# Decoder with a state-space stage on one core: gate product moved to ScalarE and GpSimd, an opening product one step later, expert tokens ahead of the quantised weights, diagonals ahead of the experts

## The chip, the core and the metric

The kernel runs on one core of a Trainium2 chip. A core has five engines that work side by side and meet only at semaphores: TensorE (PE in the rows: matrix products; PEld is its load of weights), VectorE (DVE), ScalarE (ACT), GpSimd (POOL) and SyncE (SP, which only issues DMAs). SBUF is the working memory of 128 partitions, PSUM the eight banks of 128 x 512 fp32 that TensorE writes. The metric is the time of one execution on the device in microseconds, as the median of several runs.

## The reference

Two decoder layers over x of 4 x 512 x 256 in fp32 (4 batches of 512 tokens), each sublayer followed by a norm without gain:

```python
x = ln(x + attention16(x))                  # 16 heads of 64, one zero key added
x = ln(x + cross_attention16(x, ctx, mask)) # 16 heads of 16
x = ln(x + experts(x))                      # 8 experts, 2 per token, 256 -> 1024 -> 256
x = ln(x + state_space(x))                  # 4 layers, below
x = ln(x + decoder_block(x, ctx))           # attention to itself alone, cross attention 8 heads, MLP
x = ln(x + quantised_ffn(x))                # weights to -1, 0, 1; activations to 8 bits
```

The state-space stage, which the larger part of the change is about, does in each of its 4 layers:

```python
h = rms(x, norm_w)
xi, z = split(h @ W_in.T)                   # 512 channels each
xc = silu(conv_b + sum(xp[:, k:k+L] * conv_w[:, k] for k in range(4)))
delta, Bm, Cm = split(xc @ W_x.T)           # 64, 16, 16
delta = softplus(delta @ W_dt.T + b_dt)
A = -exp(A_log)
hs = scan(exp(delta * A), delta * xc * Bm)  # over the 512 tokens, 16 states a channel
y = sum over states (hs * Cm) + D * xc
x = x + (y * silu(z)) @ W_out.T
```

The quantised weights are `clip(round(w * s), -1, 1) / s` with `s = 1 / mean(|w|)`.

## The kernel before

The program is one list of instructions an engine, in the order of the code; each waits for counters (semaphores) that other engines raise. Nothing is scheduled by a planner: the order is that of the Python loops.

**Stages.** First both attentions, batch by batch; then the experts, 39 tiles of 128 tokens in a loop (`expert`), whose weights of 3 MB each come in by three buffers; then the gathering of the experts' outputs and norm 2 of the reference, a batch at a time (`ln(b, 2)`); then the state-space stage; then the last block and the quantised part.

**Between attention and experts.** VectorE sums the raw quantised weights `w_raw` (L1865), TensorE adds the sums over partitions (L1316), VectorE takes the means (L1868), scales and rounds `w_raw` in place (L1872, twelve instructions, and L1874). ScalarE then casts them to bf16 (L887 twice, L888). These weights are used only at the very end. TensorE transposes the first 128 expert tokens into bank 4 (L1321), ScalarE copies them to `x_T` (L893), and TensorE starts the first expert (L1337 the two products, L1347 the product down).

**The state-space stage.** A sequence is one batch in one layer: 16 sequences, `i` = 0 to 15. Each has 32 steps `w`, one for each of 16 states and each half (`hf`) of the 512 channels; `W` counts steps through all sequences. In a step VectorE multiplies delta times xc by B (L1934, from PSUM bank 6 into banks 4 and 5) and scans (L1940); ScalarE makes the decays three steps ahead (L1035); GpSimd multiplies the state by C (L773, which waits for the scan); TensorE adds the product to y in banks 0 to 3 by the identity (`add_up`, L1450, two steps behind the scans) and spreads B of the next state over the partitions into bank 6 at odd steps (`spread`, L1435, which waits until both B products of the last state are done). Banks 0 and 1 hold y of half 0, banks 2 and 3 that of half 1; a sequence's y is opened by `D * xc`, a product with a diagonal matrix (`direct`, L1443).

**What runs beside it.** While sequence `i` is scanned, the engines prepare sequence `i + 1` (`start_of`: convolution as products with diagonals L1393, projections L1403, delta products L1410, z products L1364; on ScalarE and GpSimd the softplus as a series, GpSimd's L726 to L741) and the norm and first projection of `i + 2` (`opening`), and finish sequence `i - 1` (`end_of`: output product L1425 at steps 8, 10, 13, 18; `residual` L1956 on VectorE). All of it goes through bank 7. The last two sequences have no opening beside them and the last no `start_of`.

**The border of two sequences.** y of sequence `i - 1` is complete after its steps 30 and 31, which TensorE adds at steps 0 and 1 of sequence `i`. VectorE's `gated` (L1950) multiplies it by silu(z) from PSUM straight into `m_sz`, two instructions behind step 0 and two behind step 1. Only then may `direct(i, hf)` open the banks anew, at steps 1 and 2; and the output product of step 8 waits for `m_sz`.

**The diagonals.** GpSimd makes them from the identity: `conv_weights` (L708, four for each of four channel groups) and `direct_weights` (L713). For layer 0 they stand behind the gathering of the experts' outputs, for later layers beside sequences 2, 6 and 10.

## Time and profile before

| what | value |
| --- | --- |
| time, median of 3 runs | 4558.01 us (4556.92 to 4558.54) |
| the profiled execution's own time, its span | 4549.7 us, 4548.0 us |
| TensorE busy | 3853.8 us, 85% |
| VectorE busy | 3084.3 us, 68% |
| ScalarE busy | 2298.5 us, 51% |
| GpSimd busy | 2283.6 us, 50% |
| scan stage, first to last scan | 1891.1 to 3845.1 us |
| expert loop | 1333.6 to 1758 us |
| TensorE's granted clock over the execution | 0.935 of full |

Busy shares are averages over stages with different limits, so they don't say what bounds a stage. In rows with times, the first number is the start in us from the span's beginning, the second the length; `[1.50 <-PE PS L1450]` means that the engine was idle for 1.50 us before and that TensorE's line 1450 released it. `x2` after an operation merges that many. AR is the large SBUF tensor from which nearly all tiles are cut, PS is PSUM. TensorE has two clock levels, 1.2 and 2.4 GHz; a granted clock of 1.00 is the upper one.

### The profile page before, as it was taken

How to read it: one execution, taken by the hardware profiler on the slowest of the kernel's cores; microseconds unless marked ns; L12 is line 12 of the kernel's file. 1: busy time of each engine (PE TensorE's matmuls, PEld its weight loads, DVE VectorE, ACT ScalarE, POOL GpSimd, SP SyncE). 2: the span in 40 equal slices, each digit the busy share in tenths (PEclk: the TensorE clock that was granted, in tenths of full speed). 3: DMA queues.
4: the chain of work that ended last, by engine and by line, in shares of the span. 5: the costliest groups of instructions: out<-in, count | busy, mean ns of one | idle time of the engine just before them, and what ended most of it. 6: DMA issues, size and time to landing. Idle time of an engine off the chain costs nothing.

```text
span 4548.0 us, 47995 instructions
## 1 busy us (share of the span) xinstructions
PE 3853.8 (85%) x15752; PEld 2039.0 (45%) x15760; DVE 3084.3 (68%) x4131; ACT 2298.5 (51%) x4201; POOL 2283.6 (50%) x1206
## 2 busy tenths in 40 slices
PE   7878878888759996699999999999999987887786
PEld 3443443443449995233333333343433333444443
DVE  3465456446551112499999999999999998546546
ACT  3454455445432222566676666666666663332332
POOL 2353344335320004488888787778887785230220
PEclk9999999999979998899999999999999999788788
DMA  6000000000048885111111111111111121000000
GB/s 221 19 6 11 19 7 10 19 15 1 10 175 313 317 312 176 30 35 35 46 36 39 35 48 33 40 35 35 48 35 38 35 91 33 1 10 12 8 1 10
DMA packets 102383, 272.99 MB, mean 60 GB/s; under 512 B 9776, under 2 KB 55728, under 8 KB 96400
## 3 DMA queue, kind: packets, MB, share of 16 engines
q1 hardware_dynamic: 97216, 256.75, 16.9%
q0 software_dynamic: 4944, 13.51, 0.9%
q8 instruction: 110, 1.80, 0.2%
q14 instruction: 113, 0.93, 0.1%
HBM read 237.32 MB, written 32.90 MB: 59 GB/s over the span
## 4 chain that ended last, share of the span: by engine, by line
PE 36%; POOL 18%; DVE 18%; issue 17%; ACT 9%; SPq 1%; DMA 0%; POOLq 0%; DVEq 0%; ACTq 0%
POOL AR L672 11%; DVE AR L1940 8%; PE PS L1450 7%; PE PS L1337 6%; DVE PS L1934 4%; PE PS L1393 4%; POOL AR L773 3%; PE PS L1347 3%; PE PS L1169 3%; PE PS L1364 3%; ACT AR L1035 2%; PE PS L1177 2%; PE PS L1196 2%; PE PS L1209 2%; PE PS L1443 1%
## 5 line engine op out<-in xcount | busy, mean ns | idle before, releaser
L773 POOL TENSOR_TENSOR AR<-AR 128x1024 f32<-128x1024 f32 x512 | 1215.5, 2378 | 415.1 <-DVE AR L1940 338.8
L1940 DVE TENSOR_TENSOR_SCAN AR<-AR,PS 128x1024 f32<-128x1024 f32 x512 | 1170.5, 2286 | 17.6
L672 POOL TENSOR_TENSOR AR<-AR,rden 128x1024 f32<-128x1024 f32 x320 | 605.4, 1893 | 1051.0 <-DVE rden L1671 985.1
L1450 PE MATMUL PS<-AR,ident 128*128 128x512 f32 x2048 | 1022.7, 627 | 33.1 <-POOL AR L773 33.1
L1035 ACT ACTIVATE AR<-AR,mcol 128x511 f32<-128x511 f32 x1024 | 668.1, 712 | 141.2 <-DVE AR L1940 138.9
L1934 DVE TENSOR_TENSOR PS<-AR,PS 128x1024 f32<-128x1024 f32 x512 | 627.9, 1226 | 78.7 <-PE PS L1435 59.7
L1450 PEld LDWEIGHTS PS<-AR,ident 128*128 128x128 f32 x2048 | 370.8, 193 | 479.7 <-issue 412.3
L1209 PE MATMUL PS<-ident,AR 128*128 128x128 f32 x2560 | 376.5, 294 | 156.7 <-POOL AR L672 90.2
L1209 PEld LDWEIGHTS PS<-ident,AR 128*128 128x128 f32 x2560 | 299.9, 150 | 405.4 <-issue 218.6
L827 ACT ACTIVATE AR<-PS,nm 128x512 f32<-128x512 f32 x384 | 260.0, 682 | 315.6 <-DVE nm L1696 219.9
L1196 PE MATMUL PS<-AR 32*128 32x512 f32 (+1 forms) x1280 | 315.9, 705 | 45.1 <-ACT e L830 11.6
L1660 DVE COPY AR<-PS 128x512 f32<-128x512 f32 x320 | 220.4, 689 | 112.8 <-PE PS L1209 111.2
L1337 PE MATMUL PS<-AR 128*128 128x128 f32 x2496 | 287.3, 276 | 8.2 <-ACT AR L893 8.2
L1169 PE MATMUL PS<-AR 128*128 128x512 f32 x608 | 282.8, 623 | 13.2 <-ACT AR L807 4.5
L1337 PEld LDWEIGHTS PS<-AR 128*128 128x128 f32 x2496 | 286.9, 193 | 10.5 <-ACT AR L893 8.6
L1364 PE MATMUL PS<-AR 128*128 128x512 f32 x512 | 259.3, 631 | 30.8 <-ACT AR L1013 23.8
L1177 PE MATMUL PS<-AR 128*128 128x256 f32 (+1 forms) x896 | 236.8, 424 | 32.5 <-DVE AR L1734 18.0
L837 ACT ACTIVATE AR<-PS 128x512 f32<-128x512 f32 x320 | 188.9, 590 | 137.6 <-PE PS L1209 137.6
L1231 PE MATMUL PS<-AR 128*32 128x256 f32 (+1 forms) x2048 | 255.7, 451 | 2.3 <-DVE AR L1660 1.2
L1393 PE MATMUL PS<-AR 128*128 128x512 f32 x512 | 242.2, 596 | 7.6 <-ACT AR L939 3.3
L1882 DVE TENSOR_TENSOR AR<-PS,AR 128x512 f32<-128x512 f32 x78 | 54.0, 692 | 271.3 <-ACT AR L902 271.3
L1689 DVE CUSTOM_DVE_ANT_0 AR<-PS,AR 128x512 f32<-128x512 f32 x256 | 169.3, 683 | 100.6 <-PE PS L1196 99.4
(259 smaller groups left out, 4674.4 us busy)
## 6 DMA issues: line engine op xcount, KB each, us to landing
AR<-in_xw SPq DMA_DIRECT2D x39, 3072.0 KB, 10.5
AR<-mid_cs SPq DMA_DIRECT2D x256, 256.0 KB, 3.3
mid_xs<-AR SPq DMA_DIRECT2D x32, 512.0 KB, 7.8
AR<-mid_xs SPq DMA_DIRECT2D x39, 128.0 KB, 9.7
mid_ys<-AR POOLq DMA_DIRECT2D x39, 128.0 KB, 7.9
AR<-in_ctx SPq DMA_DIRECT2D x8, 512.0 KB, 5.0
AR<-in_mask SPq DMA_DIRECT2D x4, 1024.0 KB, 5.3
mid_x<-AR SPq DMA_DIRECT2D x8, 512.0 KB, 3.0
```

Of the source, the lines that this page charges most:

```text
L672: pool.tensor_tensor(probs[:, i % 4], probs[:, i % 4], rden[:, i % 4, :].rearrange("p (q o) -> p q o", o=1).to_broadcast([P, 2, 512]), ALU ...
L773: pool.tensor_tensor(m_HC[:, W % 3], m_H[:, W % 3, :].rearrange("p (c s) -> p c s", c=2), m_cb[:, n % 4:n % 4 + 1, :].to_broadcast([P, 2, ...
L1035: ins = act.activation(m_dA[:, W % 4, c, 1:512], m_dl[i % 2][:, cc, 1:512], ACT.Exp, scale=mcol[:, i // B, at:at + 1])
L1169: ins = pe.matmul(PS[:, place(PJ, b, u, 4), :], w[:, k, c * P:(c + 1) * P], xT[:, k, :], start=k == 0, stop=k == kc - 1)
L1196: ins = pe.matmul(PS[:, 2 * (e % 2) + q, :], qT[r:r + wide, h // per, t * P:(t + 1) * P], kT[r:r + wide, h // per, :], start=True, stop=True)
L1209: ins = pe.transpose(PS[:, 4 + q, c * P:(c + 1) * P], probs[:, k % 4, q, c * P:(c + 1) * P], ident[:])
L1337: ins = pe.matmul(PS[:, bank, f * P:(f + 1) * P], w[:, kc, f0:f0 + P], x_T[:, kc, :], start=kc == 0, stop=kc == KC - 1)
L1364: ins = pe.matmul(bank, mWin[:, k, c * P:(c + 1) * P], m_hT[:, k, :], start=k == 0, stop=k == KC - 1)
L1393: ins = pe.matmul(bank, dgc[:, 4 * c + k, :], m_xi[:, c, k:k + 512], start=k == 0, stop=k == 3)
L1450: ins = pe.matmul(PS[:, 2 * hf + c, :], ident[:], m_HC[:, W % 3, c, :], start=False, stop=n == NS - 1)
L1934: v.tensor_tensor(PS[:, 4:6, :], m_du[i % 2][:, 2 * hf:2 * hf + 2, :], PS[:, 6:7, :].to_broadcast([P, 2, 512]), ALU.mult).then_inc(d_bx, 1)
L1940: v.tensor_tensor_scan(m_H[:, W % 3, :], m_dA[:, W % 4].rearrange("p c s -> p (c s)"), PS[:, 4:6, :].rearrange("p c s -> p (c s)"), 0.0, A ...
```

## The change

1. **Gate.** VectorE's `gated` goes. ScalarE's new `taken_y` copies two banks of y into SBUF (128 x 1024), one half ahead of its other work of step 1 and one of step 2, into `m_t` (for the last two sequences into a delta buffer). GpSimd's new `gated` multiplies it into `m_sz`, behind its C products of steps 3 and 4. TensorE's `direct` waits for the copies (`d_yc`), its output product for GpSimd. Behind the last sequence both run without cover.
2. **Opening product.** `direct(i, 1)` goes from step 2, behind `add_up`, to step 3, behind `spread` and ahead of `add_up`.
3. **First expert tokens.** ScalarE copies `x_T` for the first expert ahead of the three casts. TensorE waits before the first expert no longer for the casts but for the means (`wmean_ok`), which have been read from bank 0.
4. **Diagonals** of layer 0 are built by GpSimd right behind the last scatter of tokens, ahead of the expert loop.
5. **Norms** of batches 2 and 3: ScalarE's roots go from steps 6 and 7 of the first preparation to steps 9 and 10, behind the first SiLU (`silus(-1)` at step 8).

```diff
+        y_of = lambda i: m_t if i < N_ITEM - 2 else m_dl[N_ITEM % 2]
...
+            for c in range(CI):
+                conv_weights(0, c)
+            direct_weights(0)
+
             with pool.Fori(0, NT_MOE // 3) as j:
...
-            for c in range(CI):
-                conv_weights(0, c)
-            direct_weights(0)
+            def gated(i, hf):
+                h2 = slice(2 * hf, 2 * hf + 2)
+                if hf == 0:
+                    pool.wait_ge(d_sz, i + 1)
+                pool.wait_ge(d_yc, 2 * i + hf + 1)
+                z = m_sz[i % 2][:, h2, :]
+                pool.tensor_tensor(z, z, y_of(i)[:, h2, :], ALU.mult).then_inc(d_yz, 1)
+
...
                     weighted(N_STEP * i + w)
+                    if i > 0 and 3 <= w < 5:
+                        gated(i - 1, w - 3)
...
+            for hf in range(2):
+                gated(N_ITEM - 1, hf)
...
+            token_T(0)
+
             act.wait_ge(q_rnd, 1)
             for c in range(KC):
                 act.activation(wgu[:, c, :], w_raw[:, 2 * F * c:2 * F * (c + 1)], ACT.Identity, bias=nround[:, 0:1])
...
-            token_T(0)
...
                 if w == 15 and j > 0:
                     act.wait_ge(d_delta, 2 * j)
+                    act.wait_ge(d_yz, 2 * i)
...
+            def taken_y(i, hf):
+                if i < N_ITEM - 2 and hf == 0:
+                    act.wait_ge(d_lin, 2 * (i + 2))
+                if i == N_ITEM - 1:
+                    act.wait_ge(d_yz, 2 * i)
+                act.wait_ge(d_y, N_STEP * (i + 1) - 1 + hf)
+                act.activation(y_of(i)[:, 2 * hf:2 * hf + 2, :], PS[:, 2 * hf:2 * hf + 2, :], ACT.Copy).then_inc(d_yc, 1)
...
-                if w == 6:
-                    ln(2, 2)
-                if w == 7:
-                    ln(3, 2)
                 if w == 8:
                     silus(-1)
+                if w in (9, 10):
+                    ln(w - 7, 2)
                 opening(-1, w)
...
+                    if i > 0 and 1 <= w < 3:
+                        taken_y(i - 1, w - 1)
...
+            for hf in range(2):
+                taken_y(N_ITEM - 1, hf)
...
-            pe.wait_ge(dve_set, 2)
+            pe.wait_ge(wmean_ok, 1)
...
-                        pe.wait_ge(d_yz, 4 * i)
+                        pe.wait_ge(d_yz, 2 * i)
...
                 if i:
-                    pe.wait_ge(d_yz, 4 * i - 2 + 2 * hf)
+                    pe.wait_ge(d_yc, 2 * i - 1 + hf)
...
+                    if w == 3:
+                        direct(i, 1)
                     if W >= 2:
                         add_up(W - 2)
-                    if 1 <= w < 3:
-                        direct(i, w - 1)
+                    if w == 1:
+                        direct(i, 0)
...
             own.link(v.tensor_scalar(wmean[:, 0:3], PS[:, 0, 0:3], 1.0 / (F * D), 1e-5, ALU.mult, ALU.max))
+            v.sem_inc(wmean_ok, 1)
...
-                for c in (2 * hf, 2 * hf + 1):
-                    v.tensor_tensor(m_sz[i % 2][:, c, :], PS[:, c, :], m_sz[i % 2][:, c, :], ALU.mult).then_inc(d_yz, 1)
...
-                    if i > 0 and w < 2:
-                        gated(i - 1, w)
...
-            for hf in range(2):
-                gated(N_ITEM - 1, hf)
```

**TensorE at the border of two sequences.** Before, from the spread of step 1 (L1435); L1450 is `add_up`, L1443 `direct`, L1393 the convolution:

```order
L1435 MATMUL PS<-AR,sel 128x512
L1450 MATMUL PS<-AR,ident 128x512 x2
L1443 MATMUL PS<-AR 128x512 x2
L1393 MATMUL PS<-AR 128x512 x2
L1450 MATMUL PS<-AR,ident 128x512 x2
L1443 MATMUL PS<-AR 128x512 x2
L1393 MATMUL PS<-AR 128x512 x2
L1435 MATMUL PS<-AR,sel 128x512
L1450 MATMUL PS<-AR,ident 128x512 x2
L1393 MATMUL PS<-AR 128x512 x2
```

And in the changed kernel, where the same four have lines 1461, 1476, 1469 and 1419:

```order
L1461 MATMUL PS<-AR,sel 128x512
L1476 MATMUL PS<-AR,ident 128x512 x2
L1469 MATMUL PS<-AR 128x512 x2
L1419 MATMUL PS<-AR 128x512 x2
L1476 MATMUL PS<-AR,ident 128x512 x2
L1419 MATMUL PS<-AR 128x512 x2
L1461 MATMUL PS<-AR,sel 128x512
L1469 MATMUL PS<-AR 128x512 x2
L1476 MATMUL PS<-AR,ident 128x512 x2
L1419 MATMUL PS<-AR 128x512 x2
```

The second `direct` has moved behind the next spread; six groups between two spreads have become five, and the next stretch has five instead of four.

**ScalarE at the start of the experts.** Before, L887 and L888 being the casts and L893 the copy of the tokens:

```order
L863 ACTIVATE g_t<-g_t 128x32
L887 ACTIVATE wgu<-AR,nround 128x2048 x2
L888 ACTIVATE wdn<-AR,nround 128x2048
L893 ACTIVATE AR<-PS 128x256
L906 UNCONDITIONAL_BRANCH
```

And in the changed kernel, with lines 908, 909 and 902:

```order
L878 ACTIVATE g_t<-g_t 128x32
L902 ACTIVATE AR<-PS 128x256
L908 ACTIVATE wgu<-AR,nround 128x2048 x2
L909 ACTIVATE wdn<-AR,nround 128x2048
L921 UNCONDITIONAL_BRANCH
```

The copy stands ahead of the three casts; the Silu of the first expert still stands behind them.

**ScalarE at the front of the scan stage.** Before: L968 copies the convolutions, L816 is a norm's root, L1019 the SiLU, L922 the squares of the next norm, L973 the copy of the projection:

```order
L968 ACTIVATE AR<-PS,mcol 128x512 x2
L816 ACTIVATE std<-mv,epsc 128x4 x2
L968 ACTIVATE AR<-PS,mcol 128x512
L1019 ACT_TABLE_LOAD
L1019 ACTIVATE AR<-AR 128x2048
L1023 ACT_TABLE_LOAD
L922 ACTIVATE AR,ss<-AR 128x256 x4
L924 ACT_TABLE_LOAD
L924 ACTIVATE rms<-ss,epsc 128x4
L925 ACT_TABLE_LOAD
L973 ACTIVATE AR<-PS 128x512
```

And in the changed kernel, with lines 983, 831, 1035, 937 and 988:

```order
L983 ACTIVATE AR<-PS,mcol 128x512 x3
L1035 ACT_TABLE_LOAD
L1035 ACTIVATE AR<-AR 128x2048
L1039 ACT_TABLE_LOAD
L831 ACT_TABLE_LOAD
L831 ACTIVATE std<-mv,epsc 128x4 x2
L937 ACTIVATE AR,ss<-AR 128x256 x4
L939 ACTIVATE rms<-ss,epsc 128x4
L940 ACT_TABLE_LOAD
L988 ACTIVATE AR<-PS 128x512
```

Both roots stand behind the SiLU; the number of table loads is the same, one of them has moved ahead of the roots.

## Rows read from the trace of the kernel before

**Rows 1.** One stretch: length, then busy (count) by engine, PE clock, DMA, GB/s.
```profile
2134.00:2256.00 122.00, 111.96 (x271) 47.16 (x270) 116.66 (x75) 80.61 (x122) 105.73 (x59) 0.99 0.18 47
```

**Rows 2.** Timeline, VectorE: start, length, engine, line, operation, [idle <-releaser], us.
```profile
2133.80 1.29 DVE L1950 TENSOR_TENSOR AR<-PS,AR 128x512 f32<-128x512 f32 x2 [1.50 <-PE PS L1450]
...
2135.01 1.22 DVE L1934 TENSOR_TENSOR PS<-AR,PS 128x1024 f32<-128x1024 f32 x1
...
2147.52 1.23 DVE L1934 TENSOR_TENSOR PS<-AR,PS 128x1024 f32<-128x1024 f32 x1 [0.57 <-PE PS L1435]
```

**Rows 3.** Timeline, TensorE, the same border.
```profile
2136.28 0.39 PE L1435 MATMUL PS<-AR,sel 64*128 64x512 bf16 x1 [0.87 <-DVE PS L1934]
...
2147.10 0.39 PE L1435 MATMUL PS<-AR,sel 64*128 64x512 bf16 x1
...
2154.48 0.39 PE L1435 MATMUL PS<-AR,sel 64*128 64x512 bf16 x1
```

**Rows 4.** Chain of waits, two pieces: start, length, what.
```profile
1833.63 1.71 ACT AR L922 x8
...
2162.29 1.24 DVE PS L1934
```

**Rows 5.** Groups of instructions: busy us, mean ns | idle before.
```profile
L773 POOL TENSOR_TENSOR AR<-AR 128x1024 f32<-128x1024 f32 x484 | 1148.9, 2378 | 374.3 <-DVE AR L1940 300.5 <-PE PS L1450 73.8
...
L939 ACT ACTIVATE AR<-PS 128x512 f32<-128x512 f32 x55 | 32.9, 598 | 126.4 <-PE PS L1364 126.4
```

**Rows 6.** Timelines, last border and stage end.
```profile
3732.57 0.39 PE L1435 MATMUL PS<-AR,sel 64*128 64x512 bf16 x1 [2.59 <-DVE PS L1934]
...
3730.08 1.29 DVE L1950 TENSOR_TENSOR AR<-PS,AR 128x512 f32<-128x512 f32 x2 [0.36 <-PE PS L1450]
...
3849.60 1.29 DVE L1950 TENSOR_TENSOR AR<-PS,AR 128x512 f32<-128x512 f32 x2 [2.22 <-PE PS L1450]
```

**Rows 7.** Timeline, start of the experts; last row, landing of their loads L516.
```profile
1332.97 0.36 ACT L893 ACTIVATE AR<-PS 128x256 f32<-128x256 f32 x1
...
1333.57 9.58 PE L1337 MATMUL PS<-AR 128*128 128x128 f32 x64 [8.16 <-ACT AR L893]
...
1339.69 1.28 ACT L902 ACT_TABLE_LOAD   x1 [6.36 <-PE PS L1337]
...
1343.20 3.62 PE L1347 MATMUL PS<-AR 128*128 128x256 f32 x16
...
DMA to landing us min/median/max: 10.0/10.5/16.4
```

**Rows 8.** VectorE beside GpSimd: line L1923, then timeline rows.
```profile
L1923 DVE TENSOR_SCALAR AR<-AR x32: 667/667/2000, 1846.5 to 3685.7; 128x1024 f32<-128x1024 f32 x32
...
1813.71 1.75 DVE L1640 TENSOR_SCALAR AR<-AR,mv,rstd 128x256 f32<-128x256 f32 x4
...
1821.43 1.38 DVE L1640 TENSOR_SCALAR AR<-AR,mv,rstd 128x256 f32<-128x256 f32 x4
...
1319.01 4.84 DVE L1872 TENSOR_SCALAR AR<-AR,wscale 128x1024 f32<-128x1024 f32 x12
...
1323.88 3.36 DVE L1874 TENSOR_SCALAR AR<-AR 128x6144 f32<-128x6144 f32 x1
```

**Rows 9.** Timeline, front of the scan stage.
```profile
1803.26 9.30 POOL L708 TENSOR_SCALAR AR<-ident,mcol 128x128 f32<-128x128 f32 x16
...
1805.76 5.37 PE L1393 MATMUL PS<-AR 128*128 128x512 f32 x8 [2.04 <-POOL AR L708]
...
1811.91 3.70 PE L1393 MATMUL PS<-AR 128*128 128x512 f32 x8 [0.78 <-ACT AR L968]
...
1820.88 0.30 ACT L816 ACTIVATE std<-mv,epsc 128x4 f32<-128x4 f32 x1
...
1828.22 0.30 ACT L816 ACTIVATE std<-mv,epsc 128x4 f32<-128x4 f32 x1 [7.04 <-DVE mv L1634]
...
1838.25 0.60 ACT L973 ACTIVATE AR<-PS 128x512 f32<-128x512 f32 x1
```

31 lines of the change are left out of this document (14 added, 17 removed).

## The prediction, on record before the run

> **What bounds the kernel now.** I read four things in this order. The page's slices show a scan stage, from 1890 to 3845 us of the span of 4548, in which TensorE, VectorE and GpSimd are all nearly full. The table by stretches gives one sequence of it [rows 1]: of 122 us VectorE is busy 116.7 and TensorE 112.0, so two engines are within 5 us of each other, and which one is late must be read place by place. Then the two timelines around step 0 of a sequence [rows 2, 3], and the chain of waits, which says who had it there [rows 4].
>
> The scans follow each other at about 3.6 us a step. At the border of two sequences VectorE stops for the gate products L1950: idle 1.50 us until TensorE's sum of step 30 is there, then a pair that moves what follows by 1.21 us (2133.80 to 2135.01), and a second pair like it one step on [rows 2]. Taken alone that is 3.9 us a sequence. But VectorE waits for TensorE again at step 4 (0.57 us, for L1435), and by the chain TensorE holds the path there and hands it to VectorE only at step 8, at 2162.29 [rows 2, 4]. TensorE's own rows show why [rows 3]: from L1435 of step 1 at 2136.28 it runs without idle to L1435 of step 3 at 2147.10 (10.82 us: the spread and six groups of some 1.72), and 7.38 us to the next, against about 7.2 us that VectorE needs for two steps. TensorE's only idle there is 0.87 us before step 1's spread, where it waits for the VectorE product behind the gate. The same 0.87 stands at all 14 borders with full TensorE work.
>
> **The gate and the second opening product.** VectorE loses 64 instructions; ScalarE gets 32 copies out of PSUM and GpSimd 32 products. TensorE's work stays: its opening product for the second half goes behind step 3's spread, so the stretch from step 1 to 3 becomes 9.1 us and the next 9.1, together 18.2 as now (10.82 + 7.38). What goes is only the idle before step 1: 14 x 0.87 = 12.2 us. The rest of VectorE's freed time turns into longer waits for L1435 at steps 4 and 6 (by the same sums some 1.7 and 2 us).
>
> The last border, into a sequence with no convolutions beside it, is different: TensorE idles 2.59 us there and VectorE leads [rows 6]. There the whole gate counts: 0.36 + 1.21 + 1.21 = 2.8 us.
>
> At the end of the stage nothing covers the longer route. Now the last gate pair takes 1.29 us [rows 6]; then it is copy plus product. The copy of two banks is bounded below by a copy of one (0.60) and above by two (1.20), the product is as wide as L773, 2.38 [rows 5]. I take 1.20, since the copy's time follows its width in these rows: 3.6 against 1.3, 2.3 us lost (bounds 1.7 and 2.3).
>
> What hides the rest. ScalarE's copies stand in its queue before the decays of steps 4 and 5, which run three steps ahead; the sum that the second waits for ends about 2137.7, so the decay of step 5 is done by 2143, and its scan comes at 2149. If that lead of 6 us were gone, each border would pay the copy, 1.2. TensorE reads the freed banks behind the sum of step 31, when the first copy is done, and at step 3 for the second. GpSimd's products at steps 3 and 4 stand before the C products L773, 2.38 us each in a step of 3.6: slack 1.2 us a step, caught up by step 9, and TensorE asks for those products two steps late. The output product at step 8 waits for the gate of step 4. Scan stage: 12.2 + 2.8 - 2.3 = 12.7 us gained.
>
> **First expert tokens ahead of the quantised weights.** Their copy L893 stands in ScalarE's queue behind three casts and starts at 1332.97; TensorE, idle for 8.16 us since it transposed the tokens, starts at 1333.57 [rows 7]. Moved ahead, the copy runs at 1325.4, right behind the transposition, and TensorE 7.5 us earlier. Its weights are there: the first expert's load is issued before the tokens' own, and the slowest load of the stage takes 16.4 us [rows 7], which is early enough for the next ones too. The casts still end at 1333.0; then come the table load (1.28), Silu (0.60), VectorE's product, and TensorE's L1347 at about 1335.8 instead of 1343.20. So 7.4 us at most.
>
> Two things eat from it. First, the diagonals run on GpSimd while VectorE quantises. VectorE's wide tensor_scalar L1923 takes 0.667 us, but once, beside a GpSimd product, 2.00; and four L1640, beside four of the very diagonals in question, took 1.75 us where four take 1.38 alone [rows 8]. That is 0.37 lost in 1.38. Quantising is 4.84 + 3.36 = 8.2 us [rows 8], so by the same ratio 2.2 us; the bounds are nothing, and one GpSimd instruction (0.60) before each of the 12 narrow ones, 7.2. I take 2.2, since it comes from these two kinds side by side. Second, TensorE now has a gap between its early products and L1347, and it fell to the 1.2 GHz level after a gap before: L1393 took 5.37 us instead of 3.70 after idle of 2.04 [rows 9]. Between nothing and 1.7; I take 0.8, the gap being near 2 again. Left: 4.4 us, bounds 0 and 7.4. The expert loop behind is TensorE without idle, so the gain is carried through it.
>
> The Trainium skill, "SBUF — State Buffer", section "Who interferes with whom", says that a VectorE instruction in a two-port mode (tensor_scalar may take one) and a GpSimd instruction exclude each other for a whole instruction. The 2.00 us row agrees with a full block; the L1640 rows show far less, 0.37 us for four. By the rule in full the expert gain would be nearly nil, which is rival 3.
>
> **Diagonals ahead of the experts.** 16 + 4 instructions of 0.60 us leave the front of the scan stage. TensorE's first convolution waits 2.04 us for the first four; a gap behind a ScalarE copy is 0.78 there, so it starts 1.3 us earlier. It may also stay at the high level, 1.7 us more [rows 9].
>
> **Norms 2 and 3 behind the first SiLU.** Now ScalarE idles 7.04 us for norm 3 before the last convolution copy at 1828.42 [rows 9]. After the change the copies and the SiLU pass at once, but the roots wait: last copy at about 1823.2 instead of 1828.4, SiLU done at 1827, two table loads, root 2 at 1829.7 instead of 1820.88. From root 2 to root 3 VectorE needs 7.34 us (1820.88 to 1828.22), so root 3 comes at 1837.1, and only then its 0.30, the squares 1.71 [rows 4], a root of 0.30, a table load 1.28 and copy L973 at 1840.7, against 1838.25 now. Late by 2.5 us, or by 0.9 if the first convolution stays fast. TensorE, idle for longer, then starts the delta products at the low level: up to 1 us more. Bounds 0.9 and 3.5 lost; I take the middle, 2.2. The 7 us of idle are not removed but moved behind the SiLU.
>
> **Sum.** 12.7 + 4.4 - 2.2 = 14.9 us off the profiled execution's 4549.7, giving 4534.8. The runs' median is 8.3 above that execution, so 4558.0 - 14.9 = 4543.1.
>
> **Rivals.**
> 1. TensorE is not the bound at the border and the whole gate counts: 15 x 3.9 = 59 us, 4499. For it: the idle is put down to the gate. Against: TensorE's gapless 18.2 us and the chain.
> 2. The two stage fronts cost their upper bounds: TensorE's clock falls wherever a gap is new, experts gain 0.5 and the norms lose 3.5, and one more dip costs the scans some us: 12.7 + 0.5 - 3.5 = 9.7 at best, 4548 to 4553.
> 3. The port excludes for whole instructions: quantising 7.2 us later, expert gain 0.2: 12.7 + 0.2 - 2.2 = 10.7, 4547.
> 4. Slower: GpSimd does not catch up. Its delta products from step 20 on already delay L773 and with it TensorE's sums. If the 4.7 us put in at steps 3 and 4 were still there at step 20, each of 15 sequences would be 4.7 longer: 15 x 4.7 - 15 = 56 slower, 4614. It decides when GpSimd's slack from step 5 to 19 is under 4.7 us; by 1.2 a step it is about 18, and in a sequence with new diagonals (9.6 us at steps 9 to 17) still 8.
> 5. The change does less than it says: step 1's product is late for another reason, ScalarE's or GpSimd's, and the 0.87 stays. Then 2.8 - 2.3 + 4.4 - 2.2 = 2.7, 4555.
>
> **How the numbers follow.** Forecast 57%, its own range 4536 to 4549. Rival 1 8%, rival 2 10%, rival 3 13%, rival 4 6%, rival 5 6%. The range 4530 to 4553 takes in rivals 2 and 3 and leaves out 1, 4 and 5. What a measurement of this kernel can tell from no change is about 0.2%, 9.1 us: faster means below 4548.9. The forecast nearly whole, rival 1 and most of 3 lie below: 0.74. Rival 2, most of 5 and the rest of 3: 0.19. Slower, by rival 4 or a cost not seen: 0.07.
>
> **What would show it.** Right: no idle of TensorE before step 1's spread; spreads 9.1 us apart twice; VectorE waiting 1.7 to 2 us for the spread at steps 4 and 6; a sequence 0.87 us shorter; the first expert product near 1326 and VectorE's quantising longer than 8.2 us; ScalarE idle some 7 us before the third norm's root. Wrong: sequences shorter by 3 us or more, GpSimd still late at step 20, or the first scan nearer to the last expert than now.

## The result, and the profile of the changed kernel

| | time, median | against the kernel before |
| --- | --- | --- |
| before, the runs beside it | 4558.01 us (4552.26 to 4566.69, 13 runs) | |
| changed kernel | 4546.84 us (4544.32 to 4552.24, 13 runs) | ratio 0.9975, 95% interval [0.9967, 0.9984]: 11 us less, 7 to 15 |
| forecast | 4543.1 us, range 4530 to 4553 | 14.9 less |
| changed kernel, measured again (`e5`) | 4534.49 us (11 runs), before 4549.23 | 0.9970 [0.9961, 0.9979]: 14 us less, 10 to 18 |

The two profiled executions are 4549.70 (before) and 4548.43 us (changed): only 1.3 us apart, since the first lies 8.3 below the median of its kernel and the second 1.6 above. The parts must therefore be compared stretch by stretch. The cuts are the same in every kernel: GpSimd's last scatter of tokens, the root of norm 0 ahead of the scan stage, the first B product, the last scan, the first residual behind it, the end.

| stretch, us | before | changed | changed again | forecast of the difference |
| --- | --- | --- | --- | --- |
| last scatter to norm's root (experts) | 465.76 | 460.02 | 460.04 | -4.4 |
| root to first B product (front) | 109.89 | 121.93 | 108.29 | +2.2 |
| first B product to last scan | 1953.00 | 1939.50 | 1939.49 | -15.0 |
| last scan to first residual | 10.18 | 13.49 | 13.39 | +2.3 |
| from there to the end | 695.01 | 695.33 | 695.45 | 0 |

The stage of the scans is the same to 0.01 us in both executions; the front is 13.6 us apart, and this alone hides the gain in the first one. One row starts it. ScalarE's copies of the projections, changed kernel (start, length, idle before and its releaser):

```profile
1791.00 0.60 ACT L954 ACTIVATE AR<-PS 128x512 f32<-128x512 f32 x1 [4.29 <-PE PS L1390]
1801.53 0.60 ACT L954 ACTIVATE AR<-PS 128x512 f32<-128x512 f32 x1 [9.93 <-remote]
```

The copy at 1801.53 comes 8 us after its product was done (TensorE's at 1791.65 took 1.98), and what released it isn't an engine of the page's list ("remote"). TensorE then works at the 1.2 GHz level:

```profile
1791.65 1.98 PE L1390 MATMUL PS<-AR 128*128 128x512 f32 x4 [1.11 <-issue]
1802.18 3.78 PE L1390 MATMUL PS<-AR 128*128 128x512 f32 x4 [8.54 <-issue]
1811.12 5.48 PE L1419 MATMUL PS<-AR 128*128 128x512 f32 x8 [0.69 <-ACT AR L954]
```

Now the border of two sequences, which answers to [rows 2, 3]. VectorE first, then TensorE's spreads:

```profile
2137.68 1.23 DVE L1963 TENSOR_TENSOR PS<-AR,PS 128x1024 f32<-128x1024 f32 x1 [0.31 <-PE PS L1461]
2154.11 1.23 DVE L1963 TENSOR_TENSOR PS<-AR,PS 128x1024 f32<-128x1024 f32 x1 [1.97 <-PE PS L1461]
2163.21 1.23 DVE L1963 TENSOR_TENSOR PS<-AR,PS 128x1024 f32<-128x1024 f32 x1 [1.97 <-PE PS L1461]
```

```profile
2137.20 0.39 PE L1461 MATMUL PS<-AR,sel 64*128 64x512 bf16 x1
2144.58 0.39 PE L1461 MATMUL PS<-AR,sel 64*128 64x512 bf16 x1
2153.68 0.39 PE L1461 MATMUL PS<-AR,sel 64*128 64x512 bf16 x1
2162.78 0.39 PE L1461 MATMUL PS<-AR,sel 64*128 64x512 bf16 x1
```

No row of TensorE there carries an idle time: the 0.87 us is gone. The spreads are 9.10 us apart twice, and VectorE waits 1.97 us for each. The pitch of the sequences falls from 123.32 to 122.40 us (the shorter ones, four before and three after, from 121.87 to 120.91), counted from step 8 to step 8: 11.7 us over the first 14 borders, and 2.2 at the last. Over the whole stage (groups of VectorE, x is the count):

```profile
L1934 DVE TENSOR_TENSOR PS<-AR,PS 128x1024 f32<-128x1024 f32 x512 | 627.9, 1226 | 78.7 <-PE PS L1435 59.7 <-DVE AR L1940 0.5
L1950 DVE TENSOR_TENSOR AR<-PS,AR 128x512 f32<-128x512 f32 x64 | 41.2, 686 | 27.2 <-PE PS L1450 26.1
L1956 DVE TENSOR_TENSOR AR<-PS,AR 128x256 f32<-128x256 f32 x63 | 25.5, 405 | 6.3 <-PE PS L1425 6.3
```

```profile
L1963 DVE TENSOR_TENSOR PS<-AR,PS 128x1024 f32<-128x1024 f32 x512 | 628.1, 1227 | 123.7 <-PE PS L1461 99.7 <-POOL AR L747 1.9 <-DVE AR L1969 0.9
L1977 DVE TENSOR_TENSOR AR<-PS,AR 128x256 f32<-128x256 f32 x63 | 25.5, 405 | 17.2 <-PE PS L1451 17.2
```

The first fence is the kernel before, the second the changed one. VectorE has lost 41.2 us of gate products and the 27.2 of idle before them. The rows of the B products hold the wait before the first of them too, 30.34 us before and 28.82 after; without it VectorE has 46.5 more of idle at the B products, and 10.9 more at the residuals (the longer end). Of 68 us freed on this engine some 11 came off the time.

The start of the experts, answering to [rows 7, 8]; VectorE, GpSimd (all 16, then the one of them that stands beside VectorE's last row), ScalarE, TensorE:

```profile
1321.49 6.11 DVE L1901 TENSOR_SCALAR AR<-AR,wscale 128x1024 f32<-128x1024 f32 x12
1327.63 3.36 DVE L1903 TENSOR_SCALAR AR<-AR 128x6144 f32<-128x6144 f32 x1
```

```profile
1317.52 14.51 POOL L694 TENSOR_SCALAR AR<-ident,mcol 128x128 f32<-128x128 f32 x16
1327.72 3.73 POOL L694 TENSOR_SCALAR AR<-ident,mcol 128x128 f32<-128x128 f32 x1
```

```profile
1327.59 0.38 ACT L902 ACTIVATE AR<-PS 128x256 f32<-128x256 f32 x1 [26.20 <-PE PS L1347]
```

```profile
1328.03 9.98 PE L1363 MATMUL PS<-AR 128*128 128x128 f32 x64 [0.47 <-ACT AR L902]
1339.62 3.72 PE L1373 MATMUL PS<-AR 128*128 128x256 f32 x16 [1.40 <-DVE AR L1911]
```

The twelve scalings take 6.11 us instead of 4.84, the rounding behind them 3.36 as before [rows 8], GpSimd's 16 diagonals, most of them beside both, 14.51 instead of 9.30 [rows 9]. The one that starts right behind the rounding (1327.63) takes 3.73 us instead of 0.59: it ends 0.46 us behind the rounding's end, so it stood for the whole of that instruction. TensorE's product down takes 3.72, so its clock did not fall in the gap of 1.40.

The end of the stage, answering to [rows 6]:

```profile
3842.74 1.98 PE L1476 MATMUL PS<-AR,ident 128*128 128x512 f32 x4 [1.60 <-POOL AR L779]
3848.36 3.07 PE L1451 MATMUL PS<-AR 128*128 128x256 f32 x8 [3.64 <-issue]
3851.95 3.78 PE L1451 MATMUL PS<-AR 128*128 128x256 f32 x8 [0.52 <-DVE AR L1977]
```

```profile
3845.92 2.34 POOL L788 TENSOR_TENSOR AR<-AR 128x1024 f32<-128x1024 f32 x1 [0.93 <-ACT AR L1047]
```

```profile
3844.82 1.02 ACT L1047 ACTIVATE AR<-PS 128x1024 f32<-128x1024 f32 x1 [2.56 <-PE PS L1476]
```

Behind the last sum (ends 3844.72) come a copy of 1.02 us and a product of 2.34, and TensorE's two first output products take 3.07 and 3.78 us instead of 1.97 and 1.99. From the last scan to the last of the four residuals it is 22.81 us instead of 17.71, 5.1 more, of which the stage's stretch in the table shows 3.3.

### The profile page after: what moved, and what is told of

Read it like the earlier page. It is cut to its first block, busy times and chain, and to the rows that moved or that the text cites. A ratio compares the mean times of both kernels' runs of the same rounds, so it can differ in the third digit from the quotient of the medians.

```text
span 4546.8 us, 48012 instructions
## 1 busy us (share of the span) xinstructions
PE 3861.4 (85%) x15752; PEld 2041.5 (45%) x15760; DVE 3044.8 (67%) x4067; ACT 2329.8 (51%) x4233; POOL 2361.3 (52%) x1238
## 3 DMA queue, kind: packets, MB, share of 16 engines
q0 software_dynamic: 4944, 13.51, 0.8%
## 4 chain that ended last, share of the span: by engine, by line
PE 38%; DVE 20%; issue 17%; POOL 17%; ACT 6%; SPq 1%; DMA 0%; POOLq 0%; DVEq 0%; ACTq 0%
POOL AR L674 11%; DVE AR L1969 9%; PE PS L1476 8%; PE PS L1363 6%; DVE PS L1963 5%; PE PS L1419 4%; PE PS L1390 3%; PE PS L1373 3%; POOL AR L779 3%; PE PS L1195 3%; PE PS L1203 2%; PE PS L1222 2%; PE PS L1235 2%; ACT AR L1059 1%; PE PS L1469 1%
## 5 line engine op out<-in xcount | busy, mean ns | idle before, releaser
L1222 PE MATMUL PS<-AR 32*128 32x512 f32 (+1 forms) x1280 | 315.0, 702 | 45.6 <-ACT e L845 12.2
```

The lines of the kernel that those rows point to most:

```text
L1222: ins = pe.matmul(PS[:, 2 * (e % 2) + q, :], qT[r:r + wide, h // per, t * P:(t + 1) * P], kT[r:r + wide, h // per, :], start=True, stop=True)
```

## The experiments

Every time is against runs of the kernel before on the same chip. "Stage" is first B product to last scan.

| run | ratio to before [95%] | experts | front | stage | last scan to residual |
| --- | --- | --- | --- | --- | --- |
| before | | 465.76 | 109.89 | 1953.00 | 10.18 |
| e1 gate alone | 0.9973 [0.9963, 0.9983] | 465.78 | 109.90 | 1939.26 | 13.51 |
| e2 tokens alone | 0.9980 [0.9971, 0.9989] | 458.66 | 109.84 | 1953.08 | 10.18 |
| e3 diagonals back | 0.9963 [0.9949, 0.9976] | 459.48 | 116.30 | 1939.79 | 13.98 |
| e4 norms back | 0.9952 [0.9939, 0.9966] | 460.72 | 104.93 | 1939.67 | 14.01 |
| e5 change again | 0.9970 [0.9961, 0.9979] | 460.04 | 108.29 | 1939.49 | 13.39 |
| e6 opening at step 2 | 0.9983 [0.9974, 0.9992] | 465.79 | 109.68 | 1939.26 | 13.36 |
| e7 no opening | 0.9869 [0.9854, 0.9884] | 459.88 | 108.21 | 1890.18 | 14.18 |
| e8 norms back, last gate VectorE | 0.9958 [0.9944, 0.9972] | 460.09 | 104.94 | 1939.83 | 10.12 |
| e9 no gate | 0.9962 [0.9948, 0.9976] | 465.77 | 109.74 | 1939.29 | 8.51 |
| e10 gate twice | 0.9982 [0.9972, 0.9992] | 460.12 | 108.23 | 1942.70 | 18.04 |
| e11 opening by GpSimd | 0.9870 [0.9854, 0.9887] | 459.78 | 109.08 | 1902.48 | 10.11 |

**e1, the gate alone** (parts 1 and 2; the rest of the diff taken back).

> Parts 1 and 2 of the change (gate by ScalarE and GpSimd, second opening product at step 3) on the kernel before; tokens, diagonals and norms stand as before. Theory (gain by TensorE's idle alone): the pitch of two sequences falls from 123.32 and 121.86 us to 122.4 and 120.9, TensorE's 0.87 before step 1's spread is gone, the end of the stage (last scan to first residual) grows from 10.2 to about 13.5 us with TensorE's output products at the low clock. From the first B product to the last residual 8 us less (not the 12.7 forecast); time 7 to 9 us under before. Start of the experts and front of the scan stage as before: first expert product near 1333.6, third norm's root within 0.3 us of the second's copy work, no stall of ScalarE before the last projection copies. Rival (the change's 11 us come from parts 3 to 5 and the scans' gain is paid back at the end): under 3 us off the time.

Stage 13.7 us shorter, end 3.3 longer, experts and front as before to 0.02 us. From the first B product to the last residual 8.6 us less (1962.09 against 1970.71), where 8 were expected; to the end of the execution about 10. By the runs it is 12 us less (8 to 17), more than the 7 to 9 expected. The rival falls.

**e2, the tokens alone.**

```diff
+            token_T(0)
             act.wait_ge(q_rnd, 1)
...
-            token_T(0)
...
-            pe.wait_ge(dve_set, 2)
+            pe.wait_ge(wmean_ok, 1)
```

> Part 3 alone on the kernel before (first expert tokens copied ahead of the casts, TensorE waits for the means). Theory (the diagonals' share of SBUF took 1.3 us of quantising): first expert product near 1326, quantising 8.2 us long instead of 9.5, second expert about 7 us earlier than before counted from the last scatter, the same to the first B product; time 6 to 7.4 us under before. Rival 1 (the gain is lost in the expert loop or behind it, where GpSimd's scatter and gathers set the end): first B product less than 3 us earlier, time within 3 us. Rival 2 (TensorE's clock falls in the new gap): second expert only 5 us earlier.

Quantising as before, and TensorE:

```profile
1326.20 10.08 PE L1337 MATMUL PS<-AR 128*128 128x128 f32 x64 [0.47 <-ACT AR L887]
1336.76 3.72 PE L1347 MATMUL PS<-AR 128*128 128x256 f32 x16 [0.26 <-DVE AR L1883]
```

7.1 us off the experts, and all of it reaches the first B product. Both rivals fall: the clock stays up across a gap of 0.26 us and, in the changed kernel, across one of 1.40.

**e3, the diagonals back behind the gathers** (the changed kernel with part 4 undone).

```diff
-            for c in range(CI):
-                conv_weights(0, c)
-            direct_weights(0)
             with pool.Fori(0, NT_MOE // 3) as j:
...
+            for c in range(CI):
+                conv_weights(0, c)
+            direct_weights(0)
             for w in range(N_STEP):
                 start_of(-1, w)
```

> The changed kernel with part 4 undone: GpSimd builds the 20 diagonals behind the gathers again. Theory (they cost little at either place): quantising back from 9.5 to 8.2 us, second expert 1.3 us earlier; TensorE waits about 2 us for the first diagonals before the first convolution and may fall to the low clock there, 1.3 to 3 us later; time within 2 us of the changed kernel, so 9 to 13 under before. Rival (ScalarE's 7.9 us standstill before its second projection copy, seen in the changed kernel's profile, comes from the diagonals' new place): the standstill is gone and the time 6 to 8 us under the changed kernel, 17 to 19 under before. If the standstill comes by chance in single executions, it stands in some of these profiles and not in others, and no time follows it.

Quantising back to 8.2 us. The front takes 116.30 against 108.29 in `e5`: in the profile the diagonals' new place is worth 8 us there, not 2. But only 2.1 of the 8 stand ahead of the x_proj product (46.0 us behind the root of norm 0 against 43.9). The rest comes behind it, from products with no diagonals in them: behind the same gaps, two more z products and one more projection run at the low level in `e3`. The third z product in `e3`, then in `e5`:

```profile
1861.67 3.78 PE L1389 MATMUL PS<-AR 128*128 128x512 f32 x4 [0.69 <-ACT AR L1028]
```

```profile
1859.78 1.98 PE L1390 MATMUL PS<-AR 128*128 128x512 f32 x4 [0.69 <-ACT AR L1029]
```

The ratios of `e3` and `e5` can't be told apart, and the cleaner pair is `e1` and `e4` below. No standstill, and so no sign that it belongs to the diagonals.

**e4, the norms back** (the changed kernel with part 5 undone).

```diff
+                if w == 6:
+                    ln(2, 2)
+                if w == 7:
+                    ln(3, 2)
                 if w == 8:
                     silus(-1)
-                if w in (9, 10):
-                    ln(w - 7, 2)
```

> The changed kernel with part 5 undone: the roots of norms 2 and 3 at steps 6 and 7 again. Theory (the move made the front later): ScalarE's idle of 7 us stands before the third norm's root and the last convolution copy, copy of x_proj's product 2 to 4 us earlier counted from the first norm's root, TensorE's x_proj and delta products not at the low clock; time 2 to 3 us under the changed kernel, 13 to 14 under before. Rival (the move is neutral, since the vector engine's norms end at the same time either way): front and time as in the changed kernel. Rival 2 (ScalarE's standstill comes from the moved norm code): standstill gone, 8 us less.

The front is 3.4 us shorter than in `e5`, as the theory says, and 5.0 shorter than in `e1`, from which it differs there by the diagonals alone; by the runs the kernel is 22 us under before, though the intervals of `e4` and `e5` overlap. What makes the 3.4 us is in TensorE's rows, here `e4` (norms early), then `e5` (late): the product of x_proj and the first delta product.

```profile
1824.03 5.54 PE L1431 MATMUL PS<-AR 128*128 128x512 f32 x8 [7.67 <-issue]
1831.14 1.12 PE L1438 MATMUL PS<-AR 64*128 64x512 f32 x2 [1.57 <-ACTq L991]
```

```profile
1816.97 5.37 PE L1429 MATMUL PS<-AR 128*128 128x512 f32 x8 [4.05 <-issue]
1831.63 2.07 PE L1436 MATMUL PS<-AR 64*128 64x512 f32 x2 [9.29 <-ACTq L991]
```

Counted from the root of norm 0 the x_proj product runs 3.6 us earlier with the norms late (43.9 against 47.5), and its successor 4.0 later (58.6 against 54.6): between them TensorE has 9.29 us of idle instead of 1.57, and the delta products take 2.07 us, at the lower clock, from the first on. In `e4` they take 1.12 and 1.73 and only then 2.07, and its x_proj product is slow too (5.54), which the theory denied. Of the 4.0 us, grown to 4.6 by the clock, a projection at the low level in `e4` gives 1.3 back.

**e5, the changed kernel once more.**

> The changed kernel itself, once more, beside the others of this call. Theory (ScalarE's 7.9 us standstill before its second projection copy comes by chance in single executions): another profile shows none, the first root of norms to the first B product takes about 114 us instead of 121.9, span some 8 us shorter than 4546.8. Rival (it belongs to this kernel's code): it stands there again at the same instruction, 121.9 us. Time against before as measured, 0.9967 to 0.9984.

The same instructions, without the standstill:

```profile
1783.30 3.78 PE L1390 MATMUL PS<-AR 128*128 128x512 f32 x4 [0.78 <-ACT AR L967]
1787.76 1.98 PE L1390 MATMUL PS<-AR 128*128 128x512 f32 x4 [0.69 <-ACT AR L954]
1795.78 3.70 PE L1419 MATMUL PS<-AR 128*128 128x512 f32 x8 [0.69 <-ACT AR L954]
```

The standstill does not belong to the code; none of the twelve other profiles used here has it. How often it comes is open: the execution that had it is only 1.6 us above the median of its kernel's runs, in a measurement where the kernel before was 9 us and the changed kernel 12 us slower than in the one of `e5`. Some of those runs, without a profile, may have stood still as well; nothing shows it. It cost 13.6 us in that execution, more than its own 7.9, because the clock fell behind it. Without it the front is 1.6 us shorter than before (108.29 here, 108.21 and 108.23 in `e7` and `e10`, whose front is the same code).

**e6, the second opening product at step 2** (`e1` with part 2 undone).

```diff
-                    if w == 3:
-                        direct(i, 1)
                     if W >= 2:
                         add_up(W - 2)
-                    if w == 1:
-                        direct(i, 0)
+                    if 1 <= w < 3:
+                        direct(i, w - 1)
```

> The gate by ScalarE and GpSimd on the kernel before, but the second opening product at step 2 behind the sum, as before (parts 1 without 2; nothing of 3 to 5). Theory (TensorE's work sets the border; where in it the product stands is worth nothing): first B product to last scan 1939.3 us as with both parts, time within 2 us of e1, 10 to 14 under before; TensorE's stretch from step 1's spread to step 3's stays 10.8 us and the next 7.4, so VectorE waits longer at step 4 and hardly at step 6. Rival (at step 2 it waits for ScalarE's second copy): TensorE idle up to 1 us at each border, first B product to last scan up to 1953, the gain of 13.5 us gone.

The stage is 1939.26 us, as in `e1` to the hundredth. VectorE's waits for the spreads of steps 4 and 6 sit otherwise, with the same sum as in the changed kernel (3.94 both):

```profile
2147.49 1.23 DVE L1961 TENSOR_TENSOR PS<-AR,PS 128x1024 f32<-128x1024 f32 x1 [3.69 <-PE PS L1462]
2154.87 1.23 DVE L1961 TENSOR_TENSOR PS<-AR,PS 128x1024 f32<-128x1024 f32 x1 [0.25 <-PE PS L1462]
```

The second product behind step 3's spread is worth nothing; TensorE's 18.2 us are the same wherever it stands. The rival falls.

**e7, no opening products** (D * xc left out of y).

```diff
-                    if w == 3:
-                        direct(i, 1)
...
-                    if w == 1:
-                        direct(i, 0)
...
                 pe.wait_ge(d_hc, W + 1)
+                if i and n == 0:
+                    pe.wait_ge(d_yc, 2 * i - 1 + hf)
                 for c in range(2):
-                    ins = pe.matmul(PS[:, 2 * hf + c, :], ident[:], m_HC[:, W % 3, c, :], start=False, stop=n == NS - 1)
+                    ins = pe.matmul(PS[:, 2 * hf + c, :], ident[:], m_HC[:, W % 3, c, :], start=n == 0, stop=n == NS - 1)
```

> The changed kernel without the opening products: D * xc is left out of y, four TensorE products less a sequence; the first sum of each half opens the bank and waits for the copy. Theory (TensorE holds the path at the borders): its gapless 18.2 us from step 1 to step 5 fall by 4 x 0.47 = 1.9 us, VectorE's waits of about 2 us at steps 4 and 6 shrink by as much together, each of 14 borders is 1.9 us shorter, first B product to last scan 1939.5 - 26 = 1913; time 24 to 28 us under the changed kernel. Rival 1 (VectorE's or GpSimd's own chain is right behind): under 7 us gained. Rival 2 (the sum of step 2 now waits for ScalarE's copy): border gains under 1 us each.

49.3 us off the stage, almost twice the 26 expected, and yet the theory's sum: I had counted four products of 0.47 us, but an opening product of a half is four instructions, 1.72 us by the starts in the rows below, which are the changed kernel's (2146.72 to 2148.44), and there are two to a border. 14 x 2 x 1.72 = 48.2.

```profile
2144.90 1.98 PE L1476 MATMUL PS<-AR,ident 128*128 128x512 f32 x4
2146.72 1.88 PE L1469 MATMUL PS<-AR 128*128 128x512 f32 x4
2148.44 1.88 PE L1419 MATMUL PS<-AR 128*128 128x512 f32 x4
```

TensorE's time at the border is the kernel's time, one to one, until VectorE's waits are used up: in `e7` they are 0.25 us there, at step 4 as at step 6:

```profile
2140.95 1.23 DVE L1961 TENSOR_TENSOR PS<-AR,PS 128x1024 f32<-128x1024 f32 x1 [0.25 <-PE PS L1461]
```

Rivals 1 and 2 fall.

**e8, the norms back** (the edit of `e4`) **and the last gate by VectorE** from PSUM.

```diff
-            for hf in range(2):
-                taken_y(N_ITEM - 1, hf)
...
-            for hf in range(2):
-                gated(N_ITEM - 1, hf)
...
+            for hf in range(2):
+                if hf == 0:
+                    v.wait_ge(d_sz, N_ITEM)
+                v.wait_ge(d_y, N_STEP * N_ITEM - 1 + hf)
+                z = m_sz[(N_ITEM - 1) % 2][:, 2 * hf:2 * hf + 2, :]
+                v.tensor_tensor(z, PS[:, 2 * hf:2 * hf + 2, :], z, ALU.mult).then_inc(d_yz, 1)
             for t in range(T):
                 residual(N_ITEM, t)
```

> The changed kernel with part 5 undone (norms 2 and 3 at steps 6 and 7) and the last sequence's gate by VectorE straight from PSUM, one instruction of 1024 columns a half. Theory: front of the scan stage 105 us as in e4; behind the last scan, sum of step 31, one VectorE product of 1.2 us, then TensorE at once: last scan to first residual 10.2 us instead of 13.5 to 14.0, and the second residual's products at the high clock, 1.8 us more; together 5 us under e4, so 0.994 of before. Rival (the low clock there comes from what stands before, not from the longer gap): 2 to 3 us under e4 only.

Last scan to first residual 10.12 us, the residuals behind it 2.09 us apart at the high clock:

```profile
3827.33 1.23 DVE L1992 TENSOR_TENSOR AR<-PS,AR 128x1024 f32<-128x1024 f32 x1 [2.29 <-PE PS L1472]
3830.66 0.43 DVE L1973 TENSOR_TENSOR AR<-PS,AR 128x256 f32<-128x256 f32 x1 [2.10 <-PE PS L1447]
3833.17 0.42 DVE L1973 TENSOR_TENSOR AR<-PS,AR 128x256 f32<-128x256 f32 x1 [2.09 <-PE PS L1447]
```

The end is mended in the profile, and the rival falls. The ratio, 0.9958, is that of `e4` within its interval: the 4 us are less than these runs can tell.

**e9, the gate left out of the kernel before** (the output product multiplies silu(z) alone).

```diff
             def gated(i, hf):
-                if hf == 0:
-                    v.wait_ge(d_sz, i + 1)
-                v.wait_ge(d_y, N_STEP * (i + 1) - 1 + hf)
-                for c in (2 * hf, 2 * hf + 1):
-                    v.tensor_tensor(m_sz[i % 2][:, c, :], PS[:, c, :], m_sz[i % 2][:, c, :], ALU.mult).then_inc(d_yz, 1)
+                return
...
-                        pe.wait_ge(d_yz, 4 * i)
+                        pe.wait_ge(d_sz, i)
...
-                if i:
-                    pe.wait_ge(d_yz, 4 * i - 2 + 2 * hf)
```

> The kernel before with the gate product left out altogether (y never meets silu(z); the output product multiplies silu(z) alone, and the opening products wait for nothing of VectorE). It is the most that taking the gate from VectorE can bring. Theory (TensorE holds the path at full borders, its only idle there is 0.87 us): 14 x 0.87 and about 1.3 to 2.8 at the last border, first B product to last scan 1938 to 1939.5 instead of 1953.0, as in the changed kernel; last scan to first residual 8.9 instead of 10.2. Time 14 to 17 us under before. Rival 1 (the whole 3.9 us of a border count): 1894, and some 60 us.

1939.29 us: the stage is as long without any gate as with the gate on ScalarE and GpSimd (1939.26 to 1939.83). So the change took all that the gate on VectorE cost, which was 13.7 us and not 3.9 a border. Rival 1 falls by the ceiling itself. The end takes 8.51 us (8.9 expected), and by the runs it is 17 us less than before (11 to 24). VectorE waits 3.68 us at step 4, as in `e6`:

```profile
2148.02 1.23 DVE L1932 TENSOR_TENSOR PS<-AR,PS 128x1024 f32<-128x1024 f32 x1 [3.68 <-PE PS L1435]
```

**e10, GpSimd's gate product twice.**

```diff
-                pool.tensor_tensor(z, z, y_of(i)[:, h2, :], ALU.mult).then_inc(d_yz, 1)
+                pool.tensor_tensor(z, z, y_of(i)[:, h2, :], ALU.mult).then_inc(d_tw, 1)
+                pool.wait_ge(d_tw, 2 * i + hf + 1)
+                pool.tensor_tensor(z, z, y_of(i)[:, h2, :], ALU.mult).then_inc(d_yz, 1)
```

> The changed kernel with GpSimd's gate product done twice (the second multiplies by y once more, so the value is another): 32 more products of 2.36 us, 4.7 us a sequence at steps 3 and 4. Theory by the sum of the prediction (slack of 18 us from step 5 to 19, 8 in a sequence with new diagonals): nothing, first B product to last scan 1939.5. Theory by the rows of the changed kernel (VectorE already waits 0.2 to 0.57 us for GpSimd's delta products before three sequences, at 2385, 2873 and 3361 us, those with diagonals, so their slack is gone): some 4.7 us at each of these three and at the last border, 14 to 19 us slower, the others unchanged. Rival 4 of the prediction (no slack anywhere): 15 x 4.7 = 70 us slower.

Right was the sum of the prediction at the full borders: the pitches are those of `e5` (122.39, and three of 120.9). The waits of VectorE for GpSimd's delta products, which the second theory put down to the sequences with new diagonals, mark the shorter pitches; these lie at the borders into sequences 4, 8 and 12 here and in the first execution of the changed kernel, and into 3, 7 and 11 in `e5`, which is the same code, so the diagonals do not fix their place. With 9.4 us of gate at steps 3 and 4 GpSimd waits for a scan again behind three further C products, at step 8:

```profile
2150.40 6.99 POOL L780 TENSOR_TENSOR AR<-AR 128x1024 f32<-128x1024 f32 x3
2158.30 2.36 POOL L780 TENSOR_TENSOR AR<-AR 128x1024 f32<-128x1024 f32 x1 [0.90 <-DVE AR L1972]
```

The waits themselves are those of the changed kernel, 1.9 us in all over the stage, and do not grow. 3.2 us are lost in the last sequence, at its steps 7 to 10, where TensorE has no work of a next sequence. GpSimd is late there: a scan waits 0.84 us for it, and TensorE, idle for 3.97 us, takes 6.51 us for eight sums that take 3.70 otherwise.

```profile
3738.68 6.51 PE L1479 MATMUL PS<-AR,ident 128*128 128x512 f32 x8 [3.97 <-POOL AR L780]
```

4.65 more are lost at the end, where nothing covers the product. The runs of this kernel scatter over 13 us, no more than those of `e5` (12) or `e11` (13). The granted clock goes with it: the four fastest runs, 4533.96 to 4538.77 us, have 0.936 or 0.937 over the execution, the other six, 4540.98 to 4547.00, have 0.934 or 0.935.

**e11, the opening on GpSimd** (`e8` with D * xc taken from TensorE; the diagonals of D go).

```diff
+            def scaled(j, hf):
+                act.wait_ge(d_du, 2 * j + hf + 1)
+                for c in (2 * hf, 2 * hf + 1):
+                    ins = act.activation(m_xc[:, c, :], m_xc[:, c, :], ACT.Copy, scale=mcol[:, j // B, M_D + c:M_D + c + 1])
+                ins.then_inc(d_xd, 1)
...
+                if n == 0:
+                    ins.then_inc(d_h1, 1)
+                    pool.wait_ge(d_h1, 2 * i + w + 1)
+                    pool.wait_ge(d_xd, 2 * i + w + 1)
+                    ins = pool.tensor_tensor(m_HC[:, W % 3], m_HC[:, W % 3], m_xc[:, 2 * w:2 * w + 2, :], ALU.add)
+                ins.then_inc(d_hc, 1)
```

ScalarE calls `scaled` at step 31 for the first half and at the next step 0 for the second; the second piece is GpSimd's `weighted`. Not shown are the edits of `e7` and a wait that keeps ScalarE from writing the next xc before GpSimd has added this one.

> The best version so far (norms at steps 6 and 7, last gate by VectorE) with the opening products taken from TensorE: ScalarE scales xc by D in place once delta * xc is made (four of 0.69 us a sequence), GpSimd adds it to its C product of the first state (two of 2.38 us a sequence at steps 0 and 1), and no D diagonals are built. Theory (TensorE holds the path, and two groups of 1.72 us of it go, as the run without them gave 49 us): first B product to last scan near 1891 to 1895 instead of 1939.8, time 40 to 48 us under the best version, about 0.985 of before. Rival (GpSimd is loaded with 5.0 us at steps 0 and 1 and with the gate's 4.7 at steps 3 and 4; with a slack of 1.2 us a step it is 5 to 6 us late at step 4, and VectorE's scans, which may run two steps ahead of it, wait): less than 15 us gained, VectorE's idle put down to GpSimd's C products at steps 3 to 8.

4490.06 us, by the ratio 59 us (1.3%) under the kernel before. The stage is 37 us shorter than in `e8`, less than the theory's 45 to 49; why, these rows don't show. The front is 4.1 us longer than in `e8`: 3.5 of them are a z product and a projection at the low level (3.71 and 3.78 us instead of 1.98 and 1.99), behind the same gaps. The rival falls. VectorE's waits over the stretch from 1900 to 3700 us, changed kernel and `e11`:

```profile
L1963 DVE TENSOR_TENSOR PS<-AR,PS 128x1024 f32<-128x1024 f32 x473 | 580.2, 1227 | 91.7 <-PE PS L1461 70.9 <-POOL AR L747 1.3 <-DVE AR L1969 0.5
```

```profile
L1973 DVE TENSOR_TENSOR PS<-AR,PS 128x1024 f32<-128x1024 f32 x484 | 593.7, 1227 | 54.5 <-PE PS L1473 30.9 <-POOL AR L746 3.9
```

The waits for TensorE fall from 70.9 to 30.9 us. GpSimd runs without a pause from step 0 to step 9 (its next wait for a scan is at 2162.10), but the scans don't wait for it there.

## Why the prediction was right, point by point

The total was forecast 3.7 us under the median measured, and 1 us from the second measurement's difference. It came out of terms of which some were off. In `e5`'s profile the stretches add up to 17.2 us gained (5.7 + 1.6 + 13.5, less 3.2 at the end and 0.4 behind it) against 14.9 forecast. The errors at the experts and the front went one way, 5.1 us, those of the stage and its end the other, 2.4. That the runs agree with the sum to 1 to 4 us is partly luck; that they can't tell 11 from 15 helps.

1. **Gate and opening product** (forecast 12.2 + 2.8 gained): 11.7 and 2.2, of which 0.4 is given back outside the borders: the stage 13.5. The mechanism is shown from both sides. Leaving the gate out gives no more than moving it (`e9`); taking 3.44 us of TensorE's work from a border gives 3.45 in the longer sequences and 3.1 in the shorter ones (`e7`). What I read as two engines within 5 us of each other [rows 1] was TensorE's place alone from step 1 to 8, as the chain [rows 4] had it. The waits came at steps 4 and 6, 1.97 us each (forecast 1.7 and 2), and 1.21 and 1.97 at three borders (into sequences 4, 8 and 12), where VectorE waits 0.20 to 0.57 us for GpSimd at step 1.
2. **End of the stage** (forecast 2.3 lost): 3.3 to the first residual. The queue part was right, 1.02 + 2.34 and their hand-overs: TensorE starts 3.64 us behind its last sum instead of 1.43 (2.2 more). Left out was the clock: after that idle time the output products took 3.07 and 3.78 us instead of 1.97 and 1.99, so that the last residual comes 5.1 us later counted from the last scan. I had put this cost in at the experts' gap and not here, where the gap was longer.
3. **GpSimd** (forecast: hidden): right, and with room for as much again at the full borders; in the last sequence that room is not there (`e10`, 3.2 us).
4. **Experts' start** (forecast 4.4 gained): 5.7. Without the diagonals 7.1 (`e2`), near the bound of 7.4. The diagonals took 1.3 us of VectorE's quantising where I took 2.2, and the clock nothing where I took 0.8. The ratio behind the 2.2 was read too broadly: of the four L1640 at 1813.71 only the first is longer, 0.74 us, and only GpSimd's last two diagonals stand beside them, so that it came near is partly luck. The larger share of the price fell on the other side, on GpSimd, 5.2 us for 16 diagonals, where nobody waits. By the Trainium skill, "SBUF — State Buffer", section "Who interferes with whom", the two exclude each other for a whole instruction; the rows agree on GpSimd's side, where one diagonal stood for the whole of the rounding (3.73 us instead of 0.59). On VectorE's side they do not show it waiting for one GpSimd instruction before each of its own, which would be 7.2 us; its 12 scalings lost 1.27. Rival 3's price falls.
5. **Front of the scan stage** (forecast 2.2 lost, bounds 0.9 to 3.5): 1.6 gained, outside the bounds. Of its two parts the norms were sized about right: without the 1.3 of the diagonals the sum has 3.8 lost and up to 1 more for the clock, and they cost 4.0 up to the first delta product, 3.4 up to the first B product (`e4` against `e5`; 6.4 by `e1` against `e3`, where the low clock lasts longer). The failing step is the diagonals, "so it starts 1.3 us earlier. It may also stay at the high level, 1.7 us more": `e4` against `e1` gives 5.0. Both named terms came (idle 2.04 to 0.69, the first convolution 3.70 instead of 5.37), and 1.8 more, since TensorE was at the high clock from the second projection product on, at 14.6 us behind the root instead of 19.1. All seven profiles with the early diagonals show that and none of the six with the late ones. Why, I can't say from the rows: the products there wait for neither GpSimd nor its diagonals. Nor does a gap settle the clock by itself. With late diagonals the first convolution took 5.37 us in three profiles and 3.67 in the other three, in `e9` behind a longer gap than the 2.04 us of [rows 9]:

```profile
1806.86 3.67 PE L1393 MATMUL PS<-AR 128*128 128x512 f32 x8 [2.10 <-POOL AR L708]
```

The front of `e9` is no shorter for it (109.74 against 109.89), since later products are slower. Only the profiled execution of the changed kernel seemed to show 12 us lost, by the standstill.
6. **Rivals.** 1 by `e9` and 3 by `e2` and the rows; 4 by `e10`; 5 by the spreads' rows. Rival 2 asked for clock dips wherever a gap is new and was half right: one came at the end of the stage and one behind the third norm, whose 3.4 us are its 3.5, but none at the experts.

What stays open: the cause of ScalarE's standstill and how often it comes, the diagonals' effect on TensorE's clock four products earlier, and with it how much of the front's 1.6 us would stay in another execution. One source of differences between executions shows: the last block, in which no kernel differs, takes from 690.8 to 699.5 us from the first residual on. The sums of its stretches in `e4` and `e11`:

```profile
sum 698.80, PE 528.84 PEld 310.31 DVE 392.49 ACT 239.05 POOL 121.12; mean PE 105.77 PEld 62.06 DVE 78.50 ACT 47.81 POOL 24.22
```

```profile
sum 691.00, PE 520.21 PEld 308.42 DVE 392.60 ACT 238.94 POOL 121.11; mean PE 104.04 PEld 61.68 DVE 78.52 ACT 47.79 POOL 24.22
```

VectorE and ScalarE are as long busy in both, TensorE 8.6 us longer in the first, and the stretch is 7.8 us longer: its granted clock rises and falls at other places (0.80 against 0.84 in the last 100 us).

## What to carry to other kernels

Take work from the engine that the chain names at the place, not from the one with the long idle row. Leaving an operation out altogether gives the ceiling of moving it, in one run: here 13.7 us of 59 that the idle rows promised. And before a stretch of one profile is blamed on a change, look whether the same stretch in a second execution agrees; here one row of 8 us, with 6 more of low clock behind it, hid the whole gain.

## What the runs showed of the hardware

- ScalarE stood still for some 7.9 us in one of thirteen profiled executions, between two copies whose inputs were ready, with the releaser "remote".
- VectorE tensor_scalars (four of 128 x 1024 and eight of 128 x 256, fp32) beside GpSimd ones of 128 x 128: 6.11 instead of 4.84 us for the twelve. GpSimd's sixteen, seven of them slowed, took 14.51 instead of 9.30, and the one that began behind the start of a VectorE tensor_scalar of 3.36 us took 3.73.
- TensorE fell to the 1.2 GHz level after 3.64 us of idle behind lightly filled work (3.07 and 3.78 us for what takes 1.98), and not after 1.40 us behind a full stretch (3.72 against 3.62). In the front of the scan stage products behind equal gaps ran at either level: 5.37 us after 2.04 of idle, 3.67 after 2.10.
- A copy of 128 x 1024 fp32 out of PSUM by ScalarE takes 1.02 us, not the 1.20 of two copies of 512.
